# A macaron block with a Mamba-2 mixer on one core: x's rows and Silu earlier in each mixer block

## The chip, the core and the metric

The kernel runs on one core of one Trainium2 chip. The metric is the device time of one launch in microseconds (us), as the median of a few runs. The core has five engines that run their own instruction streams and meet at semaphores: TensorE (PE in the profile, its weight loads PEld), VectorE (DVE), ScalarE (ACT), GpSimd (POOL) and SyncE (SP, which here only issues DMAs).

## The reference

The input is 4 sequences of 512 tokens, 512 wide. Three layers follow each other, each on a layer norm of the residual and each added to it. The first and the last are the same feed-forward (weights turned by Hadamard transforms, 2048 hidden columns, halved output), the one between is a Mamba-2 mixer:

```python
x = x + 0.5 * ffn(layernorm(x))
x = x + mixer(layernorm(x))
x = x + 0.5 * ffn(layernorm(x))

# mixer, cut
gate, xBC, dt = split(h @ in_proj_w.T)
xBC = silu(causal_conv4(xBC) + conv_b)        # x (1024), B (128), C (128)
dt = clip(softplus(dt + dt_bias), 0, 100)     # 64 heads of 16 columns
Y_diag = ((C @ B.T) * exp(segsum(A * dt))) @ (x * dt)     # within a chunk of 64
states = B.T @ (x * dt * decay_to_end)        # per chunk, then carried over chunks
Y_off  = (C @ states) * exp(cumsum(A * dt))
y = (Y_diag + Y_off + D * x) * silu(gate)
out = rmsnorm(y) * norm_w @ out_proj_w.T

# ffn
h = silu(x_gate) * x_up
```

## The kernel before

`begin` turns the weights and runs the first feed-forward of the first sequences. `mixer` is the rest, some 1310 us. Its main loop runs over the 4 sequences (q = 0 to 3) and, within one, over 8 blocks (b = 0 to 7) of 128 x columns, that is 8 heads. Each block also carries one chunk (256 of the 2048 hidden columns) of the feed-forward of another sequence, as filler for TensorE; `at = 8 * q + b` counts both. After block 7 comes a passage that prepares the next sequence; after q = 3, 16 feed-forward chunks are left without a mixer beside them. There are 32 mixer blocks: 8 to a sequence.

Nothing is scheduled at run time. The order of the instructions on each engine is the order in which the loops call the helpers, and each helper waits for the semaphores it needs. Every float32 product of the projections and of the feed-forward is made of three passes of split operands (`PASSES`), so a projection of one 128-column block is 12 matmuls of 128x512.

The helpers that matter here, in TensorE's order in a block of before:

- `x_rows` (L1287): 4 transposes of x's Silu output `xc` into bank X, whose readers on DVE are `scaled` (L1805) and `scaled_end` (L1814)
- `decay` (L1277), four times, each followed by ACT's Exp (L1552), with the four `down` matmul groups of the filler (L1231) between
- `in_proj` (L1146) for the next block's x, `new_states` (L1315), `times_start` (L1322, the product behind the carried exponents), then `up0` and `gate1` of the filler (L1190, 24 matmuls; in block 0 only 12, since `up0` stands earlier)
- `ydiag`, the inner product (L1299, 32 products, each on 32 columns of the array), `from_states`, the product from the states (L1328), `in_proj` for the next block's gate (L1146), `up1`, in odd blocks `out_proj` (L1259), and `gate0` of the next chunk (L1190)

On DVE: `states` (L1831 to L1837), `conv` of the next block (L1791, three steps), `hidden` (L1762), `hidden_low` (L1768), `within` (L1850), `carried` (L1857), and pieces of layer-norm statistics and of the mixer's own norm (L129 to L167) as they come due: `norm` in block 1 of q = 1 to 3, a piece of `other` in block 4 of q = 0 to 2, a piece of `following` in block 6 of every q. On ACT: `times` (L1557, Exp), `x_silu` (L1502), `gate` (L1521) and `silu` (L1537, all Silu), `hidden_high` (L1543), `square` (L1572). Exp and Silu sit in different function tables, so each block has two table loads (ACT_TABLE_LOAD).

Of the kernel before, what the change touches and what calls it, by code (L numbers as in the profile page):

```python
# [862 lines left out]
def mixer(nc, s, ug_s, dn_s, wsc, in_s, out_s, cum_m, cum_s, out):  # L863
# [17 lines left out]
    with ExitStack() as ctx:  # L881
# [233 lines left out]
        def _(pe):  # L1115
# [163 lines left out]
            def x_rows(q, b):  # L1279

                pe.wait_ge(s_xcv, LCONV * q + 2 + b + 1)
                if b == 0:
                    pe.wait_ge(s_gt, q + 1)
                else:
                    pe.wait_ge(s_ex, NB * q + b)
                for i in range(NPC):
                    ins = pe.transpose(X[:, ck(i)], xc[:, b % 2, ck(i)], I)  # L1287
                ins.then_inc(s_X, 1)
# [92 lines left out]
            for q in range(BATCH):  # L1381
                more = q < BATCH - 1
                for b in range(NB):
                    at = NC * q + b
                    end = b == NB - 1
                    pair = last_pair(q, b)
                    x_rows(q, b)
                    decay(q, b, 0)
                    if at == 0:
                        in_proj(q, 5, 0)  # L1390
                        decay(q, b, 1)
                        in_proj(q, 5, 1)
                        decay(q, b, 2)
                        new_states(q, b)
                        decay(q, b, 3)
                    elif b == 0:
                        in_proj(q, 5, 0)
                        decay(q, b, 1)
                        in_proj(q, 5, 1)
                        decay(q, b, 2)  # L1400
                        new_states(q, b)
                        decay(q, b, 3)
                        up0(at)
                    else:
                        down(at - 1, 0, last_pair(q, b - 1) + 1)
                        if end:
                            turn_tile(q + 1, 0)
                        down(at - 1, 1)
                        decay(q, b, 1)
                        down(at - 1, 2)  # L1410
                        if end:
                            turn_tile(q + 1, 1)
                        decay(q, b, 2)
                        down(at - 1, 3)
                        if end:
                            turn_tile(q + 1, 2)
                        decay(q, b, 3)
                        if b == 1 and q:
                            sums(q - 1)
                        if not end:  # L1420
                            in_proj(q, 5 + 2 * b)
                    if b:
                        new_states(q, b)
                    if end:
                        turn_tile(q + 1, 3)
                    times_start(q, b)
                    if b:
                        up0(at)
                    if end and more:
                        in_proj(q + 1, 0)  # L1430
                    if at:
                        gate1(at)
                    if at == 0:
                        gate0(at + 1, 0)
                    ydiag(q, b)
                    from_states(q, b)
                    if not end:
                        in_proj(q, 6 + 2 * b)
                    elif more:
                        in_proj(q + 1, 1)  # L1440
                    if at:
                        up1(at)
                    if pair >= 0:
                        out_proj(pair, at)
                    if at and (not end or not more):
                        gate0(at + 1, pair + 1)
# [3 lines left out]
                at = NC * q + NB - 1  # L1450
# [16 lines left out]
            for at in range(NC * BATCH, NC * ITEMS):  # L1467
                q, b = at // NC, at % NC
# [20 lines left out]
        def _(act):  # L1489
# [165 lines left out]
            for q in range(BATCH):  # L1655
                more = q < BATCH - 1
                for b in range(NB):
                    at = NC * q + b
                    end = b == NB - 1
# [9 lines left out]
                    if not end:  # L1669
                        raw(q, 3 + b, b + 1)  # L1670
                    times(q, b)
                    if at:
                        hidden_high(at, 0)
                    if end and more:
# [3 lines left out]
                    if end and more:  # L1678
                        step_exp(q + 1)
                        raw(q + 1, 0, NB)  # L1680
                    if at:
                        silu(at, 1)
                    if not end:
                        x_silu(q, b + 1)
                        gate(q, b + 1)
                    elif more:
                        b_silu(q + 1)
# [48 lines left out]
        def _(dve):  # L1736
# [214 lines left out]
            for q in range(BATCH):  # L1951
# [3 lines left out]
                for b in range(NB):  # L1955
# [28 lines left out]
                        keep_sums(q - 1)  # L1984
                    if end:
                        turn_tile(q + 1, 3)
                    if b == 4 and more:
                        next(other)
                    if b == 6:
                        next(following)  # L1990
                    states(q, b)
                    if not end:
                        conv(q, 3 + b, b + 1)
                    if at:
                        hidden(at, 0)
                        hidden_low(at, 0)
                    if end and more:
                        step_abs(q + 1)
                        step_one(q + 1)
                        step_rest(q + 1)  # L2000
                    within(q, b)
                    carried(q, b)
                    if end and more:
                        conv(q + 1, 0, NB)
# [195 lines left out]
```

## Time and profile before

| what | value |
|---|---|
| median of 3 runs | 1646.36 us (1646.13 to 1650.44) |
| the profiled execution | 1646.44 us, span 1644.6 us |
| TensorE busy | 98% of the span, granted clock 0.999 |
| DVE, ACT, POOL busy | 63%, 38%, 23% |
| chain that ended last | 74% PE |
| one mixer block | 27.6 us (even), 33.1 us (odd, with `out_proj`) |

The span runs from the first to the last instruction; 1.8 us of the execution lie around it. The page puts busy time, idle time and who ended it beside each line of the kernel. Matmuls overlap in the pipeline, so two starts of successive groups tell more than their durations.

### The profile page before, as it was taken

The numbers are of one execution on the slowest core, as the hardware profiler recorded it, in microseconds if no ns is written. First come the engines' busy times: TensorE is split into PE (matmuls) and PEld (weight loads), VectorE is DVE, ScalarE is ACT, GpSimd is POOL, SyncE is SP. The second block draws the span as 40 slices with busy tenths as digits, with TensorE's granted clock in tenths as the row PEclk, the third lists the DMA queues.
The fourth block names the chain that finished last, engine by engine and source line by source line (L and its number), as shares of the span: only waits on it lengthen the run. The fifth ranks groups of instructions, "written<-read, shape, count | busy, mean of one in ns | idle before, by whom it ended". The sixth has DMA issues, their size and how long they took to land.

```text
span 1644.6 us, 25044 instructions
## 1 busy us (share of the span) xinstructions
PE 1619.7 (98%) x9672; PEld 1312.1 (80%) x9672; DVE 1035.5 (63%) x2022; ACT 626.1 (38%) x934; POOL 379.1 (23%) x298
## 2 busy tenths in 40 slices
PE   6999999999999999999999999999999999999999
PEld 3788888877888778888877888877888878888887
DVE  6544445776677877777776777777775684543333
ACT  4333434463333463333464334265333341122111
POOL 1656663011221212122122122122122121000000
PEclk9999999999999999999999999999999999999999
DMA  9746564754544444454445445445444447566763
GB/s 291 298 148 245 203 222 166 268 183 143 170 156 151 154 162 145 156 168 151 150 146 167 158 148 173 157 129 195 156 156 157 156 126 223 167 181 192 214 203 129
DMA packets 253427, 290.46 MB, mean 177 GB/s; under 512 B 14464, under 2 KB 211200, under 8 KB 244096
## 3 DMA queue, kind: packets, MB, share of 16 engines
q1 hardware_dynamic: 253312, 288.88, 53.8%
q8 instruction: 78, 1.28, 0.3%
q14 instruction: 37, 0.30, 0.1%
HBM read 238.51 MB, written 50.33 MB: 176 GB/s over the span
## 4 chain that ended last, share of the span: by engine, by line
PE 74%; DVE 2%; ACT 1%; issue 1%; DMA 0%; SPq 0%; ACTq 0%; DVEq 0%
PE bank L1190 31%; PE bank L1231 14%; PE bank L1146 12%; PE bank L1259 5%; PE bank L1328 3%; PE bank L1299 2%; PE bank L1315 2%; PE bank L1277 2%; PE bank L1287 1%; PE bank L1322 1%; DVE xT L1749 0%; PE bank L1174 0%; DVE res L1775 0%; PE bank L1156 0%; DMA cum_stay<-m_aS 0%
## 5 line engine op out<-in xcount | busy, mean ns | idle before, releaser
L1190 PE MATMUL bank<-fxT,wj 128*128 128x512 f32 x1752 | 415.2, 390 | 0.0
L1190 PEld LDWEIGHTS bank<-fxT,wj 128*128 128x128 f32 x1752 | 328.6, 188 | 68.6
L1231 PE MATMUL bank<-m_wd,m_hb 128*128 128x512 f32 x1128 | 278.8, 392 | 0.0
L1231 PEld LDWEIGHTS bank<-m_wd,m_hb 128*128 128x128 f32 x1128 | 209.2, 188 | 44.8 <-issue 2.4
L1543 ACT CAST m_hb<-xn 128x512 fp32r<-128x512 f32 x96 | 59.5, 620 | 452.6 <-DVE xn L1762 452.6
L1146 PE MATMUL bank<-xT,wi 128*128 128x512 f32 x900 | 222.9, 395 | 1.6 <-DVE m_cv L1791 0.5
L1146 PEld LDWEIGHTS bank<-xT,wi 128*128 128x128 f32 x900 | 166.1, 188 | 39.6 <-issue 5.1
L1775 DVE TENSOR_TENSOR res<-bank,res 128x512 f32<-128x512 f32 x192 | 132.5, 690 | 83.0 <-PE bank L1231 80.9
L2098 POOL TENSOR_TENSOR m_L<-m_L,m_GT 128x512 f32<-128x512 f32 x36 | 52.7, 1464 | 431.9 <-ACT m_L L1552 431.9
L1762 DVE SCALAR_TENSOR_TENSOR xn<-bank,sc,xn 128x512 f32<-128x512 f32 x96 | 71.8, 747 | 121.7 <-PE bank L1190 121.6
L1537 ACT ACTIVATE xn<-bank,sc 128x512 f32<-128x512 f32 x96 | 66.1, 688 | 146.4 <-PE bank L1190 140.9
L1552 ACT ACTIVATE m_L<-bank 128x512 f32<-128x512 f32 x128 | 76.5, 598 | 83.7 <-PE bank L1277 83.4
L1768 DVE TENSOR_TENSOR m_hb<-xn,m_hb 128x512 fp32r<-128x512 f32 x96 | 66.3, 691 | 53.5 <-ACT m_hb L1543 53.5
L508 PE MATMUL bank<-xT,b_wu 128*128 128x512 f32 x384 | 95.4, 397 | 0.0
L1791 DVE SCALAR_TENSOR_TENSOR m_cv<-bank,pr,m_cv 128x511 f32<-128x511 f32 (+2 forms) x117 | 87.3, 747 | 10.5 <-ACT m_cv L1497 7.7
L508 PE MATMUL bank<-b_xT,b_wu 128*128 128x512 f32 x384 | 92.9, 392 | 0.0
L1259 PE MATMUL bank<-m_wo,m_yh 128*128 128x512 f32 x384 | 90.7, 391 | 0.7 <-ACT xn L1537 0.7
L2125 POOL TENSOR_TENSOR m_ss<-m_ss,m_y 128x512 f32<-128x512 f32 x28 | 36.2, 1294 | 239.6 <-ACT m_y L1572 239.6
L549 PE MATMUL bank<-b_wd,b_hb 128*128 128x512 f32 x384 | 90.9, 392 | 0.0
L508 PEld LDWEIGHTS bank<-xT,b_wu 128*128 128x128 f32 x384 | 71.8, 188 | 17.9 <-DVE xT L722 0.6
L1259 PEld LDWEIGHTS bank<-m_wo,m_yh 128*128 128x128 f32 x384 | 71.6, 188 | 17.7 <-issue 1.9
L508 PEld LDWEIGHTS bank<-b_xT,b_wu 128*128 128x128 f32 x384 | 72.1, 188 | 16.2 <-issue 0.7
(224 smaller groups left out, 2319.2 us busy)
## 6 DMA issues: line engine op xcount, KB each, us to landing
wj<-ug_split SPq DMA_DIRECT2D x167, 512.0 KB, 4.2
m_wd<-dn_split SPq DMA_DIRECT2D x48, 1024.0 KB, 4.8
wi<-in_split SPq DMA_DIRECT2D x76, 512.0 KB, 3.3
ug_split<-b_wu SPq DMA_DIRECT2D x8, 2048.0 KB, 14.3
m_wo<-out_split SPq DMA_DIRECT2D x32, 512.0 KB, 4.1
wi<-ug_split SPq DMA_DIRECT2D x25, 512.0 KB, 4.2
in_split<-b_msp SPq DMA_DIRECT2D x20, 512.0 KB, 4.0
raw<-in_wug SPq DMA_DIRECT2D x8, 1024.0 KB, 7.0
```

The lines of the kernel that those rows point to most:

```text
L508: ins = pe.matmul(U[j][:], wu[c % 2][:, a, k, ck(j)], xT[g][:, b, k, :], start=(k == 0 and i == 0), stop=(k == KH - 1 and i == 2))
L549: ins = pe.matmul(down_bank(n, t)[:], hb[:, n % 2, a, j, ck(t)], wd[c % 2][:, b, j, :], start=(j == 0 and i == 0), stop=(j == 1 and i == 2))
L1146: ins = pe.matmul(to[:], w[:, a, k, :], xT[:, b, k, :], start=(k == 0 and i == 0), stop=(k == KH - 1 and i == 2))
L1190: ins = pe.matmul(to[:], w[:, a, k, :], frm[:, b, k, :], start=(k == 0 and i == 0), stop=(k == KH - 1 and i == 2))
L1231: ins = pe.matmul(F[t % 2][:], hb[:, a, j, ck(t)], wd[:, b, j, :], start=(j == 0 and n == 0), stop=(j == 1 and n == 2))
L1259: ins = pe.matmul(F[1 - t % 2][:], yh[:, (2 * pair + i) % 4, a, ck(t)], wout[i][:, b, :], start=(i == 0 and n == 0), stop=(i == 1 and n == 2))
L1537: act.activation(hf[:, j, :], F[1][:], ACT.Silu, scale=sc[:, at % NC, j:j + 1]).then_inc(s_sil, 1)
L1552: act.activation(L[:, b % 2, j, :], A[:], ACT.Exp).then_inc(s_L, 1)
L1762: dve.scalar_tensor_tensor(hf[:, j, :], F[0][:], sc[:, at % NC, 2 + j:3 + j], hf[:, j, :], ALU.mult, ALU.mult).then_inc(s_h, 1)
L1768: dve.tensor_tensor(hb[:, 1, j, :], hf[:, j, :], hb[:, 0, j, :].bitcast(F32), ALU.subtract).then_inc(s_lo, 1)
L1775: dve.tensor_tensor(r, frm[:], r, ALU.add).then_inc(s_acc, 1)
L1791: ins = dve.scalar_tensor_tensor(to[:, d:SEQ], frm[:, 0:SEQ - d], pr[:, w + 3 - d:w + 4 - d], to[:, d:SEQ], ALU.mult, ALU.add)
```

## The change

In 27 of the 32 blocks (all but the last of each sequence and the very first), `x_rows` for the next block stands right behind `from_states` instead of at the head of the next block, and `ydiag` stands right behind `times_start` instead of behind `gate1`. On ACT, `x_silu` comes straight after `times`, ahead of the filler's second Silu, `hidden_high` and `square`. On DVE, `states` and `conv` come ahead of the statistics pieces of blocks 4 and 6, and `hidden_low` comes behind `within`. No instruction is added or removed.

```diff
 # tensor
-                    x_rows(q, b)
+                    if b == 0 or at == 1:
+                        x_rows(q, b)
@@
                     times_start(q, b)
+                    if at and not end:
+                        ydiag(q, b)
@@
-                    ydiag(q, b)
+                    if at == 0 or end:
+                        ydiag(q, b)
                     from_states(q, b)
+                    if at and not end:
+                        x_rows(q, b + 1)
 # scalar
                     times(q, b)
+                    if at and not end:
+                        x_silu(q, b + 1)
+                        silu(at, 1)
                     if at:
                         hidden_high(at, 0)
@@
-                    if at:
+                    if at == 0:
+                        x_silu(q, b + 1)
+                    elif end:
                         silu(at, 1)
                     if not end:
-                        x_silu(q, b + 1)
                         gate(q, b + 1)
 # vector
+                    states(q, b)
+                    if not end:
+                        conv(q, 3 + b, b + 1)
                     if b == 4 and more:
                         next(other)
                     if b == 6:
                         next(following)
-                    states(q, b)
-                    if not end:
-                        conv(q, 3 + b, b + 1)
                     if at:
                         hidden(at, 0)
+                    if end:
                         hidden_low(at, 0)
@@
                     within(q, b)
+                    if at and not end:
+                        hidden_low(at, 0)
                     carried(q, b)
```

TensorE in an even block of before, from the new states to the first decay of the next block:

```order
L1315 MATMUL bank<-m_xd,m_Bt 128x128 x7
L1322 MATMUL bank<-m_aS,m_i2x 128x512
L1190 MATMUL bank<-fxT,wj 128x512 x24
L1299 MATMUL bank<-m_L,m_xp 32x64 x32
L1328 MATMUL bank<-m_Cf,m_sta 128x64 x7
L1146 MATMUL bank<-xT,wi 128x512 x12
L1190 MATMUL bank<-fxT,wj 128x512 x24
L1287 MATMUL bank<-cs,m_xc 128x128 x4
L1277 MATMUL bank<-m_mvg,m_stn 128x512
```

The same place now:

```order
L1315 MATMUL bank<-m_xd,m_Bt 128x128 x7
L1322 MATMUL bank<-m_aS,m_i2x 128x512
L1299 MATMUL bank<-m_L,m_xp 32x64 x32
L1190 MATMUL bank<-fxT,wj 128x512 x24
L1328 MATMUL bank<-m_Cf,m_sta 128x64 x7
L1287 MATMUL bank<-cs,m_xc 128x128 x4
L1146 MATMUL bank<-xT,wi 128x512 x12
L1190 MATMUL bank<-fxT,wj 128x512 x24
L1277 MATMUL bank<-m_mvg,m_stn 128x512
```

`ydiag` (L1299) moved ahead of the 24 filler matmuls, the four transposes (L1287) moved ahead of the gate's projection and of 24 more.

ScalarE in a block of before, from the carried exponents' Exp to the filler's next Silu, with the semaphores that each row waits for (`ms_cv` is `conv`, `ms_y` is `within`, `gate` and `ms_flo` belong to the filler):

```order
L1557 ACTIVATE m_ex<-bank 128x512 [waits ms_yf,ms_E]
L1543 CAST m_hb<-xn 128x512 [waits ms_fd,ms_fh]
L1572 ACTIVATE m_y<-m_y 128x512 [waits ms_yl]
L1537 ACT_TABLE_LOAD [waits ms_flo]
L1537 ACTIVATE xn<-bank,sc 128x512 [waits gate]
L1502 ACTIVATE m_xc<-m_cv 128x512 [waits ms_cv,ms_y,ms_X]
L1521 ACTIVATE m_zs<-bank 128x512 [waits ms_yf,projected]
```

The same place now (line numbers are those of the changed kernel: L1563 is `times`, L1508 `x_silu`, L1543 `silu`, L1549 `hidden_high`, L1578 `square`, L1527 `gate`):

```order
L1563 ACTIVATE m_ex<-bank 128x512 [waits ms_yf,ms_E]
L1508 ACT_TABLE_LOAD [waits ms_cv,ms_y]
L1508 ACTIVATE m_xc<-m_cv 128x512 [waits ms_X]
L1543 ACTIVATE xn<-bank,sc 128x512 [waits ms_flo,gate]
L1549 CAST m_hb<-xn 128x512 [waits ms_fd,ms_fh]
L1578 ACTIVATE m_y<-m_y 128x512 [waits ms_yl]
L1527 ACTIVATE m_zs<-bank 128x512 [waits ms_yf,projected]
```

The Silu table's load, which stood behind `square`, now stands behind `times`, and `conv` and `within` are waited for ahead of it.

VectorE in block 1 of q = 1 now, where the mixer's norm begins (L1772 is `hidden`, L1860 `within`, L1778 `hidden_low`, L1867 `carried`, L129 and L130 the norm's first steps):

```order
L1772 SCALAR_TENSOR_TENSOR xn<-bank,sc,xn 128x512
L1860 SCALAR_TENSOR_TENSOR m_y<-m_xc,pr,bank 128x512
L1778 TENSOR_TENSOR m_hb<-xn,m_hb 128x512
L1867 TENSOR_TENSOR m_ex<-bank,m_ex 128x448
L129 TENSOR_SCALAR m_rr<-m_rr 128x4
L130 TENSOR_SCALAR m_rr<-m_rr 128x4
```

Before, `hidden_low` stood ahead of `within`; the rest is as it was.

## Rows read from the trace of the kernel before

**Rows 1.** Page, part 1: engine, busy us, share, instructions.

```profile
PE 1619.7 (98%) x9672; PEld 1312.1 (80%) x9672; DVE 1035.5 (63%) x2022; ACT 626.1 (38%) x934; POOL 379.1 (23%) x298
```

**Rows 2.** Timeline, block 3 of q = 1: start us, us, instruction, [idle before, releaser].

```profile
703.55 0.50 PE L1322 MATMUL bank<-m_aS,m_i2x 128*128 128x512 f32 x1
703.89 5.62 PE L1190 MATMUL bank<-fxT,wj 128*128 128x512 f32 x24
...
707.77 2.31 DVE L1791 SCALAR_TENSOR_TENSOR m_cv<-bank,pr,m_cv 128x511 f32<-128x511 f32 x3
709.45 1.10 PE L1299 MATMUL bank<-m_L,m_xp 128*32 128x64 f32 x64
710.48 1.77 PE L1328 MATMUL bank<-m_Cf,m_sta 128*128 128x64 f32 x14
712.06 3.01 PE L1146 MATMUL bank<-xT,wi 128*128 128x512 f32 x12
...
725.85 0.60 PE L1287 MATMUL bank<-cs,m_xc 128*128 128x128 f32 x4
...
726.52 2.91 PE L1231 MATMUL bank<-m_wd,m_hb 128*128 128x512 f32 x12
```

**Rows 3.** Timeline, end of block 4 of q = 2.

```profile
1004.37 2.31 DVE L1791 SCALAR_TENSOR_TENSOR m_cv<-bank,pr,m_cv 128x511 f32<-128x511 f32 x3
...
1004.95 1.77 PE L1328 MATMUL bank<-m_Cf,m_sta 128*128 128x64 f32 x14
1006.79 0.76 PEld L1146 LDWEIGHTS bank<-xT,wi 128*128 128x128 f32 x4 [0.21 <-issue]
```

**Rows 4.** Timeline, two table loads and what the waits beside them were for.

```profile
358.81 0.71 PE L1363 MATMUL bank<-cs,m_L 64*128 64x64 f32 x8
359.60 1.28 ACT L1552 ACT_TABLE_LOAD   x1 [0.29 <-PE bank L1363]
...
368.23 1.28 ACT L1502 ACT_TABLE_LOAD   x1
370.94 2.31 DVE L1791 SCALAR_TENSOR_TENSOR m_cv<-bank,pr,m_cv 128x511 f32<-128x511 f32 x3
373.28 0.63 ACT L1502 ACTIVATE m_xc<-m_cv 128x512 f32<-128x512 f32 x1 [3.77 <-DVE m_cv L1791]
```

**Rows 5.** Timeline, block 0 of q = 2.

```profile
881.15 2.31 DVE L1791 SCALAR_TENSOR_TENSOR m_cv<-bank,pr,m_cv 128x511 f32<-128x511 f32 x3
...
884.24 3.01 PE L1146 MATMUL bank<-xT,wi 128*128 128x512 f32 x12
```

**Rows 6.** Timeline, block 1 of q = 2.

```profile
908.39 2.31 DVE L1791 SCALAR_TENSOR_TENSOR m_cv<-bank,pr,m_cv 128x511 f32<-128x511 f32 x3
...
913.31 0.62 DVE L1857 TENSOR_TENSOR m_ex<-bank,m_ex 128x448 f32<-128x448 f32 x1
...
918.87 0.75 DVE L1762 SCALAR_TENSOR_TENSOR xn<-bank,sc,xn 128x512 f32<-128x512 f32 x1
...
919.67 0.99 PEld L1259 LDWEIGHTS bank<-m_wo,m_yh 128*128 128x128 f32 x5 [0.32 <-DVE xn L1762]
```

**Rows 7.** Page, part 5: line, tiles, count, busy us, mean ns, idle before.

```profile
L1543 ACT CAST m_hb<-xn 128x512 fp32r<-128x512 f32 x96 | 59.5, 620 | 452.6 <-DVE xn L1762 452.6
L1537 ACT ACTIVATE xn<-bank,sc 128x512 f32<-128x512 f32 x96 | 66.1, 688 | 146.4 <-PE bank L1190 140.9
L1768 DVE TENSOR_TENSOR m_hb<-xn,m_hb 128x512 fp32r<-128x512 f32 x96 | 66.3, 691 | 53.5 <-ACT m_hb L1543 53.5
```

**Rows 8.** Timeline, from block 6 to block 7 of q = 2.

```profile
1078.34 1.28 ACT L1552 ACT_TABLE_LOAD   x1
...
1079.63 0.60 ACT L1552 ACTIVATE m_L<-bank 128x512 f32<-128x512 f32 x1
...
1080.28 0.19 PEld L1277 LDWEIGHTS bank<-m_mvg,m_stn 128*128 128x128 f32 x1 [0.63 <-ACT m_L L1552]
```

## The prediction, written before the changed kernel ran

> **What bounds the kernel now.** I read the page's busy shares first: TensorE is busy for 98% of the span, every other engine for less than two thirds [rows 1]. Most of the 25 us in which it is idle lie ahead of the mixer. So a block is as long as TensorE's own stream, and a change of order can only remove small waits of TensorE or add some. I then read the timeline of one block, start of group to start of group [rows 2]. The 24 filler matmuls start 0.34 us after `times_start` and take 5.56 us, 0.23 each; `ydiag` takes 1.03 us to the next group's start, `from_states` 1.58, and nothing idles between. `conv` ends at 710.08, two microseconds before the gate's projection at 712.06, whose bank it has to free. In blocks 4 and 6 a piece of statistics stands ahead of `states` on DVE, so `conv` ends at 1006.68 and the projection's weights wait: 1.84 us after the start of `from_states` where the normal block has 1.58 [rows 2, 3]. That is about 0.27 us, in 7 blocks (4 and 6 of q = 0 to 2, 6 of q = 3).
>
> **ydiag behind times_start.** The same 32 products and the same two changes of the array's tile, one in and one out. The trace has no change from the long matmul of `times_start` to 32-column tiles. Behind the filler, `ydiag` starts 0.06 before the modelled end of the last matmul (703.89 + 5.62 against 709.45); by the same rule it would start at 703.55 + 0.50 - 0.06, 0.44 behind `times_start`, and the filler 1.03 after that, with its first weights exposed as now (0.34 rather than 0.23 to the next). The fillers then run straight into `from_states` without a tile change. Sum to the start of `from_states`: 0.44 + 1.03 + 0.11 + 24 x 0.23 = 7.1, against 6.93 now, whose own first weights (some 0.05 to 0.1) are hidden afterwards. I take 0. Bounds: nothing, or a loss of 0.1 a block, that is 2.4 us in 24; a gain needs the next point's wait to leave room, and it doesn't.
>
> **x's rows earlier.** At the head of a block the four transposes cost 725.85 to 726.52 less the 0.23 that the decay matmul alone takes: 0.44 us [rows 2]. They cost the same 0.44 behind `from_states`. Moved work is neutral where TensorE is bound, except where a later wait is fixed by something else (block 7, below). Their release, though, now comes from a new chain: `conv`, then ACT. DVE's readers of the rows (`scaled`) start earlier, off the path.
>
> **The table load.** This decides the sign. In before, the Silu table is loaded behind `square`, at a time when nobody waits for ACT. Now the load stands between `times` and `x_silu`, and the order puts the waits for `conv` and `within` ahead of it, with only bank X's on the Silu itself. The trace shows both arrangements. Where no wait stands ahead, the load ran at 368.23 while `conv` ended only at 373.25, and the Silu started 0.03 later. Where the wait stands ahead, the load began 0.08 after the product it was waiting for (358.81 + 0.71, then 359.60) [rows 4]. So I take it that the 1.28 us are spent after `conv`. The x rows' weights then come at the end of `conv` + 0.08 + 1.28 + 0.02 + 0.63 + 0.05 (the lag of weights behind `hidden` in block 1: 919.62, 919.67 [rows 6]) = 2.06 us.
>
> - Normal blocks, and 4 and 6, where the statistics now stand behind `conv`: it ends 6.53 after `times_start` [rows 2], the weights come at 8.59. `from_states`, starting at 7.0, would let them start at 8.55. A wait of 0.04 in 21 blocks: +0.8.
> - Block 0 of q = 1 to 3 has only 12 filler matmuls ahead. `conv` ends at 883.46, the weights come at 885.52, and TensorE is there at 884.24 [rows 5]. 1.28 us; I take 1.25 in 3 blocks: +3.8.
> - Block 1 of q = 1 to 3 has the mixer's norm on DVE, a chain of tiny steps between `carried` (ends at 913.93) and the second `hidden` (918.87), and TensorE already waits 0.32 for that `hidden`, less the usual 0.05 [rows 6]. Now `carried` stands behind `hidden_low`, which needs `hidden_high`, which stands behind both Silus on ACT: `conv` ends at 910.70, load until 912.06, x's Silu until 912.70, the filler's (0.69, overlapping by 0.1) until 913.29, `hidden_high` (0.62, overlapping) until 913.81, `hidden_low` (0.69) until 914.53, `carried` until 915.08 [rows 6, 7]. That is 1.15 late, `hidden` too, and TensorE gives back 0.44 of it at the head of the next block: +0.7 in 3 blocks, +2.1.
>
> What is queued behind the load on ACT in other blocks has room: the filler's second Silu ended at 10.37 after `times_start` in before and would end near 9.1 now; `hidden_high` goes from 7.8 to 9.6, and what needs it first is a `down` eight microseconds off.
>
> **Blocks 4 and 6.** The 0.27 goes in 7 blocks: -1.9. What is late next there is the 0.04 above, counted.
>
> **Block 6 to 7.** At the head of block 7 TensorE waits for the first decay's Exp (1079.63 + 0.60), and its next weights start 0.05 later, 0.63 after the ones before [rows 8]. That Exp follows the filler's Silu, two row copies and a table load, a chain fixed by `gate0`'s end. The 0.44 taken out in front of it only lengthens the wait, while block 6 has already paid for the rows: +0.44 in 4 sequences, +1.8. In the other blocks the same Exp has about half a microsecond to spare; after the shift it would release the weights some 0.1 late, and a weight load is given out well ahead of the end of the matmul before it, so that such a delay need not reach the stream. I take 0.3 in all; between 0 and 1.9 (0.1 in 19 blocks).
>
> **Sum.** 0 + 0.8 + 3.8 + 2.1 - 1.9 + 1.8 + 0.3 = +6.9 us on the profiled execution's 1646.44 (span 1644.6 and 1.8 around it), which is the median of 1646.36 to within 0.1. Forecast 1653.3.
>
> SyncE's loads are the same; some are released about a microsecond later, since the fillers end later, and each lands long before its use.
>
> **Rivals.**
>
> A, the load runs ahead: ACT's queue issues it while `conv` still runs. Then x's Silu ends 0.65 after `conv`, block 0 has no wait (weights at 884.16 against 884.24), and block 1's DVE chain keeps its time, so that its present 0.27 wait is covered by the 0.44. Sum: -1.9 + 1.8 - 0.8 + 0.3 = -0.6, that is 1645.8: not slower. It decides if the load starts before `conv` ends. For it speaks 368.23; against it that no wait stood ahead there. Chance 0.14.
>
> B, TensorE pays more: the tile change behind `times_start` costs 0.1 more in 24 blocks (+2.4), and the late first decay 0.1 in 19 (+1.9). 6.9 + 2.4 + 1.6 = +10.9: 1657.3. Nothing in the rows excludes it; chance 0.15.
>
> C, a table switch that costs more than its row. "ScalarE: Activation LUTs", section "What ACT_TABLE_LOAD costs", of the Trainium skill puts a drain of 1380 ns behind the load of 1283 ns. By that rule x's Silu would end 1.38 later in 27 blocks, +37 us: 1690. The row of 1.28 agrees with the load, and the Exp behind the load at 1078.34 starts at 1079.63, 0.01 after its end [rows 8], so the trace doesn't bear the drain out. Chance 0.01.
>
> D, the moved waits pay off: the earlier rows free DVE sooner and take a wait of TensorE that the timeline books as busy. With A's conditions this could give 1640. TensorE's idle time in the mixer is a few microseconds, so there is little to take. Chance 0.03.
>
> The forecast's own case has 0.67 and a range of 1650 to 1656.
>
> **How the numbers follow.** A measurement of this kernel tells 0.3% (4.9 us) from no change, so slower begins at 1651.3. The forecast's case lies beyond it with four parts in five (0.54), B and C do wholly (0.16): 0.69 slower with rounding. Same: the rest of the forecast's case (0.13) and A (0.14), 0.28 with a little of D. Faster: 0.03. The range for 8 in 10 takes A in at the bottom and B at the top: 1645 to 1658.
>
> **What would show it.** In the profile after: ACT's load between `times` and x's Silu starting 0.1 after `conv`; TensorE's weights for the x rows released by ACT, with an idle of over a microsecond in block 0 of three sequences and near nothing elsewhere; the wait for `hidden` in `out_proj` of block 1 grown from 0.3 to about 1; the projection's idle in blocks 4 and 6 gone; the wait at the first decay of block 7 grown from 0.6 to about 1. A load that starts right behind `times` makes the forecast wrong, and a normal block longer than 27.6 us makes it too low.

## The result, and the profile after

The changed kernel is slower: 1657.78 us, median of 4 runs (1657.23 to 1658.45), against 1646.7 of the kernel before beside it. The ratio is 1.0064, with an interval of 1.005 to 1.0077. The profiled execution took 1658.01 us (span 1656.2, granted clock .999 of full speed, as before), so the trace can be read against the span before, 1644.6: there are 11.6 us to find, where 6.9 were forecast.

The busy shares of the page's part 1 tell hardly anything of it:

```profile
PE 1624.2 (98%) x9672; PEld 1313.5 (79%) x9672; DVE 1022.3 (62%) x2022; ACT 625.2 (38%) x934; POOL 377.1 (23%) x298
```

The instructions are the same in number, and still TensorE's busy time grew by 4.5 us [rows 1], so only 7.1 of the 11.6 us stand in the trace as idle time. That matmuls which wait inside a group are booked as busy would explain it; no run shows it by itself. The list of TensorE's waits (line, releaser: us in total, times, longest) shows the new ones. In it L1287 is `x_rows`, L1231 `down`, L1259 `out_proj`, L1277 `decay`, L1772 the filler's `hidden`, L1778 `hidden_low`:

```profile
PE bank L1231 <- DVE m_hb L1778: 4.2, 10, 0.7
PE bank L1287 <- ACT m_xc L1508: 3.3, 3, 1.1
PE bank L1277 <- DMA m_stn<-cum_stay: 1.4, 2, 0.9
PE bank L1259 <- DVE xn L1772: 1.5, 3, 0.5
```

The same list of before has neither of the first two. The view that settles the sizes is the distance from one `times_start` to the next, block by block, in the timelines, taken from the starts of its weight load (PEld L1322). A block thus reaches into the head of the next. Means over q = 1 to 3 (block 4: q = 1 and 2, the sequences with statistics in it), in us:

| | block 0 | 1 | 2 | 3 | 4 | 5 | 6 |
|---|---|---|---|---|---|---|---|
| before | 25.83 | 33.26 | 27.56 | 33.05 | 27.84 | 33.05 | 28.12 |
| after | 27.10 | 33.96 | 28.50 | 33.11 | 28.17 | 33.12 | 28.32 |

Summed over their blocks: block 0 +3.8, block 1 +2.1, block 2 +2.8, block 4 +1.0, block 6 +0.8 (four times), the other moved blocks +0.7 in all. Block 7 of q = 2 is 1.0 longer through a DMA's round trip, the row L1277 above, whose wait goes from execution to execution (0.8 in before, 1.4 here, 2.4 in one experiment that doesn't touch it). Together +12.2; the stretch up to the first `times_start` was 0.7 shorter (365.3 against 366.0), where TensorE's wait for a start-up load fell from 11.5 to 10.5. That leaves about the 11.6 us of the span.

**Block 0.** Timeline of q = 2: start us, us, instruction, [idle before, releaser], as in all timelines below. L1801 is `conv`, L1508 `x_silu`:

```profile
882.25 0.40 PE L1322 MATMUL bank<-m_aS,m_i2x 128*128 128x512 f32 x1
...
884.86 2.30 DVE L1801 SCALAR_TENSOR_TENSOR m_cv<-bank,pr,m_cv 128x511 f32<-128x511 f32 x3
...
887.26 1.28 ACT L1508 ACT_TABLE_LOAD   x1 [3.98 <-DVE m_cv L1801]
888.55 0.63 ACT L1508 ACTIVATE m_xc<-m_cv 128x512 f32<-128x512 f32 x1
...
889.24 0.42 PEld L1287 LDWEIGHTS bank<-cs,m_xc 128*128 128x128 f32 x4 [1.23 <-ACT m_xc L1508]
```

`conv` ends at 887.16. ACT, idle for 4 us, starts the load 0.10 later and the Silu 1.29 after that; TensorE stands for 1.23 us. In [rows 5] it went from `from_states` straight into the projection. The Silu begins 0.01 us behind the load: the drain of 1380 ns that the Trainium skill's "ScalarE: Activation LUTs" ("What ACT_TABLE_LOAD costs") puts there does not show.

**Block 1.** q = 2. L1543 is the filler's Silu, L1549 `hidden_high`, L1778 `hidden_low`, L1867 `carried`, L1772 the second `hidden`:

```profile
915.74 1.28 ACT L1508 ACT_TABLE_LOAD   x1 [5.49 <-DVE m_cv L1801]
917.04 0.63 ACT L1508 ACTIVATE m_xc<-m_cv 128x512 f32<-128x512 f32 x1
917.58 0.67 ACT L1543 ACTIVATE xn<-bank,sc 128x512 f32<-128x512 f32 x1
918.14 0.61 ACT L1549 CAST m_hb<-xn 128x512 fp32r<-128x512 f32 x1
918.78 0.69 DVE L1778 TENSOR_TENSOR m_hb<-xn,m_hb 128x512 fp32r<-128x512 f32 x1 [1.83 <-ACT m_hb L1549]
919.39 0.62 DVE L1867 TENSOR_TENSOR m_ex<-bank,m_ex 128x448 f32<-128x448 f32 x1
...
924.94 0.75 DVE L1772 SCALAR_TENSOR_TENSOR xn<-bank,sc,xn 128x512 f32<-128x512 f32 x1
...
925.74 1.01 PEld L1259 LDWEIGHTS bank<-m_wo,m_yh 128*128 128x128 f32 x5 [0.93 <-DVE xn L1772]
```

The chain conv, load, two Silus, `hidden_high`, `hidden_low`, `carried` runs as forecast, DVE stands 1.83 us in it, and the wait in `out_proj` is 0.93 where it was 0.32 [rows 6].

**Block 2.** This one was not forecast. Here VectorE has `ending` (L1931, the end of the norm of the q before) between `carried` and the second `hidden`; the list of pieces under "The kernel before" doesn't have it. On GpSimd L2138 is `add_squares`, which waits for ACT's `square`, and L2126 and L2128 are `combine`:

```profile
952.76 0.69 DVE L1778 TENSOR_TENSOR m_hb<-xn,m_hb 128x512 fp32r<-128x512 f32 x1 [1.82 <-ACT m_hb L1549]
953.34 1.28 POOL L2138 TENSOR_TENSOR m_ss<-m_ss,m_y 128x512 f32<-128x512 f32 x1 [10.54 <-ACT m_y L1578]
953.37 0.62 DVE L1867 TENSOR_TENSOR m_ex<-bank,m_ex 128x448 f32<-128x448 f32 x1
953.91 5.22 DVE L1931 SCALAR_TENSOR_TENSOR res<-m_acc,m_rr,res 128x512 f32<-128x512 f32 x4
954.58 1.61 POOL L2126 TENSOR_TENSOR m_y<-m_y,m_ex 128x448 f32<-128x448 f32 x1
956.27 1.62 POOL L2128 TENSOR_TENSOR m_y<-m_y,m_zs 128x512 f32<-128x512 f32 x1
959.05 0.74 DVE L1772 SCALAR_TENSOR_TENSOR xn<-bank,sc,xn 128x512 f32<-128x512 f32 x1
...
961.42 1.39 PE L1231 MATMUL bank<-m_wd,m_hb 128*128 128x512 f32 x5 [0.65 <-DVE m_hb L1778]
```

In before, block 2 of q = 2 starts at 937.41, and the same place reads (L1921 is `ending`, L1762 `hidden`):

```profile
947.09 4.70 DVE L1921 SCALAR_TENSOR_TENSOR res<-m_acc,m_rr,res 128x512 f32<-128x512 f32 x4
951.76 0.75 DVE L1762 SCALAR_TENSOR_TENSOR xn<-bank,sc,xn 128x512 f32<-128x512 f32 x1
```

So `ending` begins 9.68 us after the block's start in before and 10.82 (953.91 less 943.09) in after, and takes 0.52 longer; `hidden` begins 14.35 after it in before and 15.96 in after, 1.6 later. Of the 0.52, the first of `ending`'s four steps has 0.53: taken by itself it lasts 0.74 in before and 1.27 here, since `add_squares`, now behind the load and both Silus, still runs until 954.62. `down` needs `hidden`'s low half at once, and TensorE stands 0.65 us for it.

**Block 4.** Of q = 2, behind `carried`. L137 to L139 are the tiny steps of the block's second piece of statistics, which stands where it stood before:

```profile
1015.95 1.29 POOL L2138 TENSOR_TENSOR m_ss<-m_ss,m_y 128x512 f32<-128x512 f32 x1 [11.56 <-ACT m_y L1578]
1016.51 0.75 DVE L137 TENSOR_TENSOR m_mv<-m_mv 128x4 f32<-128x4 f32 x1
1017.20 1.14 POOL L2126 TENSOR_TENSOR m_y<-m_y,m_ex 128x448 f32<-128x448 f32 x1
1017.29 1.07 DVE L138 TENSOR_TENSOR m_mv<-m_mv 128x4 f32<-128x4 f32 x1
1018.40 0.16 DVE L139 SCALAR_TENSOR_TENSOR m_mv<-m_mv 128x4 f32<-128x4 f32 x1
1018.42 1.30 POOL L2128 TENSOR_TENSOR m_y<-m_y,m_zs 128x512 f32<-128x512 f32 x1
1018.60 1.15 DVE L137 TENSOR_TENSOR m_mv<-m_mv 128x4 f32<-128x4 f32 x1
...
1020.30 0.75 DVE L1772 SCALAR_TENSOR_TENSOR xn<-bank,sc,xn 128x512 f32<-128x512 f32 x1
...
1022.68 1.62 PE L1231 MATMUL bank<-m_wd,m_hb 128*128 128x512 f32 x6 [0.33 <-DVE m_hb L1778]
```

The wait for `conv` of [rows 3] is gone, and one of 0.33 in front of a matmul of `down` has come. The second piece takes 3.8 us here (1016.51 to 1020.30) and 3.3 in before (1009.83 to 1013.09): in both it meets `combine`, and here its first step meets `add_squares` as well, 0.75 where it took 0.15.

**Block 6 to 7**, q = 2. L1558 is the first decay's Exp:

```profile
1083.99 1.63 PE L1231 MATMUL bank<-m_wd,m_hb 128*128 128x512 f32 x6 [0.33 <-DVE m_hb L1778]
...
1086.87 0.60 ACT L1558 ACTIVATE m_L<-bank 128x512 f32<-128x512 f32 x1
1087.51 0.19 PEld L1277 LDWEIGHTS bank<-m_mvg,m_stn 128*128 128x128 f32 x1 [0.50 <-ACT m_L L1558]
```

The wait behind the first decay's Exp is 0.50, against the 0.63 of [rows 8]; e7_rows_back tells what it would be without the earlier rows.

### The profile page after: what moved, and what is told of

The parts are those of the page before. It is cut to its first block, busy times and chain, and to the rows that moved or that the text cites. A ratio compares the mean times of both kernels' runs of the same rounds, so it can differ in the third digit from the quotient of the medians.

```text
span 1656.2 us, 25044 instructions
## 1 busy us (share of the span) xinstructions
PE 1624.2 (98%) x9672; PEld 1313.5 (79%) x9672; DVE 1022.3 (62%) x2022; ACT 625.2 (38%) x934; POOL 377.1 (23%) x298
## 3 DMA queue, kind: packets, MB, share of 16 engines
q8 instruction: 78, 1.28, 0.3%
## 4 chain that ended last, share of the span: by engine, by line
PE 62%; DVE 11%; issue 3%; ACT 3%; DMA 0%; SPq 0%; ACTq 0%; DVEq 0%
PE bank L1190 24%; PE bank L1231 14%; PE bank L1146 10%; PE bank L1259 5%; DVE m_cv L1801 2%; PE bank L1328 2%; DVE m_sta L1845 2%; PE bank L1315 2%; DVE m_sta L1847 1%; PE bank L1277 1%; PE bank L1299 1%; DVE res L1931 1%; PE bank L1287 1%; DVE xn L1772 1%; ACT m_hb L1549 1%
## 5 line engine op out<-in xcount | busy, mean ns | idle before, releaser
L1231 PE MATMUL bank<-m_wd,m_hb 128*128 128x512 f32 x1128 | 279.9, 394 | 4.2 <-DVE m_hb L1778 4.2
L1231 PEld LDWEIGHTS bank<-m_wd,m_hb 128*128 128x128 f32 x1128 | 208.3, 188 | 52.9 <-issue 10.7
L1785 DVE TENSOR_TENSOR res<-bank,res 128x512 f32<-128x512 f32 x192 | 132.5, 690 | 112.6 <-PE bank L1231 109.5
L1549 ACT CAST m_hb<-xn 128x512 fp32r<-128x512 f32 x96 | 59.3, 618 | 300.7 <-DVE xn L1772 300.7
L1772 DVE SCALAR_TENSOR_TENSOR xn<-bank,sc,xn 128x512 f32<-128x512 f32 x96 | 71.8, 748 | 116.5 <-PE bank L1190 116.2
L1543 ACT ACTIVATE xn<-bank,sc 128x512 f32<-128x512 f32 x96 | 65.6, 683 | 140.0 <-PE bank L1190 134.5
L1778 DVE TENSOR_TENSOR m_hb<-xn,m_hb 128x512 fp32r<-128x512 f32 x96 | 66.4, 691 | 72.1 <-ACT m_hb L1549 71.6
L1558 ACT ACTIVATE m_L<-bank 128x512 f32<-128x512 f32 x128 | 76.6, 599 | 79.1 <-PE bank L1277 78.8
L2138 POOL TENSOR_TENSOR m_ss<-m_ss,m_y 128x512 f32<-128x512 f32 x28 | 36.2, 1292 | 273.0 <-ACT m_y L1578 273.0
L1801 DVE SCALAR_TENSOR_TENSOR m_cv<-bank,pr,m_cv 128x511 f32<-128x511 f32 (+2 forms) x117 | 87.3, 746 | 10.5 <-ACT m_cv L1503 7.7
L1259 PE MATMUL bank<-m_wo,m_yh 128*128 128x512 f32 x384 | 91.1, 391 | 2.3 <-DVE xn L1772 1.5
L1259 PEld LDWEIGHTS bank<-m_wo,m_yh 128*128 128x128 f32 x384 | 71.6, 188 | 19.7 <-DVE xn L1772 2.8
```

The source lines that it names most:

```text
L1231: ins = pe.matmul(F[t % 2][:], hb[:, a, j, ck(t)], wd[:, b, j, :], start=(j == 0 and n == 0), stop=(j == 1 and n == 2))
L1259: ins = pe.matmul(F[1 - t % 2][:], yh[:, (2 * pair + i) % 4, a, ck(t)], wout[i][:, b, :], start=(i == 0 and n == 0), stop=(i == 1 and n == 2))
L1549: act.copy(hb[:, 0, j, :], hf[:, j, :]).then_inc(s_hi, 1)
L1558: act.activation(L[:, b % 2, j, :], A[:], ACT.Exp).then_inc(s_L, 1)
L1772: dve.scalar_tensor_tensor(hf[:, j, :], F[0][:], sc[:, at % NC, 2 + j:3 + j], hf[:, j, :], ALU.mult, ALU.mult).then_inc(s_h, 1)
L1778: dve.tensor_tensor(hb[:, 1, j, :], hf[:, j, :], hb[:, 0, j, :].bitcast(F32), ALU.subtract).then_inc(s_lo, 1)
```

## The experiments

Each is timed beside the kernel before, and its ratio is to that; it is worked out from the single runs, and is not the quotient of the two medians. Block lengths of all (us, as in the table above; block 5 of e9_spread is of q = 1 and 2):

| | 0 | 1 | 2 | 3 | 4 | 5 | 6 |
|---|---|---|---|---|---|---|---|
| e1_warm | 25.79 | 33.02 | 27.54 | 33.03 | 28.17 | 33.02 | 28.25 |
| e2_late | 27.08 | 33.92 | 29.31 | 33.08 | 27.91 | 33.10 | 28.29 |
| e3_ydiag | 25.84 | 33.25 | 27.59 | 33.08 | 27.84 | 33.08 | 28.10 |
| e4_conv | 25.83 | 33.25 | 27.56 | 33.05 | 28.32 | 33.05 | 27.88 |
| e7_rows_back | 25.84 | 34.38 | 28.52 | 33.08 | 28.17 | 33.08 | 27.85 |
| e8_conv_b6 | 25.83 | 33.25 | 27.56 | 33.05 | 27.83 | 33.05 | 27.88 |
| e9_spread | 25.83 | 33.06 | 27.56 | 33.06 | 27.75 | 33.93 | 28.25 |

### e1_warm: the table is called for before the wait

The changed kernel, with a Silu of one column between `times` and `x_silu`. It waits for nothing of `conv`, so the load runs early.

```diff
+        warm = sb("warm", [P, 1])
 ...
                     if at and not end:
+                        act.activation(warm[:], pr[:, P_DTB:P_DTB + 1], ACT.Silu)
                         x_silu(q, b + 1)
                         silu(at, 1)
```

> The changed kernel with one extra Silu of one column, on constant data, between times and x_silu in the 27 blocks, so that the Silu table is loaded without waiting for conv. Theory (the load behind conv is the cost): the load starts right behind times, x's Silu ends 0.7 after conv; the wait in block 0 of q = 1 to 3 goes (1.25 each, 3.8), block 1 falls from 33.9 to 33.0 and block 2 from 28.5 to 27.6 since carried is 1.2 earlier (2.8 each in three sequences), and 0.04 in the rest; blocks 4 and 6 stay, since there hidden_high waits for the first hidden, not for ACT. About 10 us less than the changed kernel: 1648. Rival (TensorE's stream itself costs more in the new order): all blocks stay as they are, 1657 to 1658. Second rival (the waits of blocks 2 and 4 are VectorE's own work): only blocks 0 and 1 give, 6.7 us less, 1651.

Measured: 1646.86 us, 10 runs, against 1645.55; 1.0002 (0.9993 to 1.0011). Span 1645.4. Block 0 of q = 2 (L1680 is the helper that records the one-column Silu, L1509 `x_silu`):

```profile
880.55 1.28 ACT L1680 ACT_TABLE_LOAD   x1
881.84 0.20 ACT L1680 ACTIVATE m_warm<-pr 128x1 f32<-128x1 f32 x1
882.08 2.31 DVE L1803 SCALAR_TENSOR_TENSOR m_cv<-bank,pr,m_cv 128x511 f32<-128x511 f32 x3
884.50 0.63 ACT L1509 ACTIVATE m_xc<-m_cv 128x512 f32<-128x512 f32 x1 [2.46 <-DVE m_cv L1803]
885.18 0.42 PEld L1288 LDWEIGHTS bank<-cs,m_xc 128*128 128x128 f32 x4
```

The load ends before `conv` starts, the rows' weights have no wait, and blocks 0, 1 and 2 are back where they were, block 1 0.24 below. Blocks 3 and 5 lose their 0.06 and 0.07 too. The span is 10.8 us shorter than the change's 1656.2. So one load, standing behind a wait, carries nearly all of the loss; the earlier rows by themselves cost nothing in those blocks. Block 4 stays long: that is another cause.

### e2_late: the statistics behind hidden_low

The changed kernel, with `ending` in block 2 and the last piece in block 4 moved behind the second `hidden_low`.

```diff
-                    if b == 2 and q:
-                        ending(q - 1)
-                    if b in (3, 4) and more:
+                    if b == 3 and more:
                         next(other)
-                    if b == 4 and more:
-                        bias(1, s_fs)
 ...
                         hidden_low(at, 1)
+                    if b == 2 and q:
+                        ending(q - 1)
+                    if b == 4 and more:
+                        next(other)
+                        bias(1, s_fs)
```

> The changed kernel with two pieces of VectorE's side work put behind the second hidden_low of their block: ending in block 2 of q = 1 to 3, and the last statistics piece with its bias in block 4 of q = 0 to 2. Theory (TensorE's wait at the first down of the next block is for the second hidden_low, which these pieces push back): block 2 falls from 28.5 to 27.65, block 4 from 28.2 to 27.65, blocks 0 and 1 stay at 27.1 and 33.9; about 4.3 us less than the changed kernel, 1653.5. Rival (the wait at that down has another cause, the late conv chain on ACT alone): nothing moves, 1657.8.

Measured: 1659.25 us, 4 runs, against 1645.55; 1.0082 (1.0067 to 1.0097). A miss: not 4 us better than the change but as slow or slower. Block 2 of q = 2 (L1815 is `scaled`, L1785 `add_down`):

```profile
959.57 0.75 DVE L1772 SCALAR_TENSOR_TENSOR xn<-bank,sc,xn 128x512 f32<-128x512 f32 x1 [3.93 <-PE bank L1190]
...
961.62 2.73 DVE L1931 SCALAR_TENSOR_TENSOR res<-m_acc,m_rr,res 128x512 f32<-128x512 f32 x4
964.27 1.72 DVE L1815 TENSOR_TENSOR m_xp<-bank,m_dd 64x256 f32<-64x256 f32 x4
966.02 0.69 DVE L1785 TENSOR_TENSOR res<-bank,res 128x512 f32<-128x512 f32 x1
...
966.76 1.24 PEld L1231 LDWEIGHTS bank<-m_wd,m_hb 128*128 128x128 f32 x6 [1.71 <-DVE res L1785]
```

`hidden` is now free of `ending`: it waits for TensorE's bank. But the next bank that `down` writes is freed by `add_down`, which stands behind `ending` and `scaled`, and the weights of TensorE's next `down` wait 1.71 us for it. In block 4 the smaller piece did gain, 0.26. Block 2 is 1.75 us longer than its old length where the change cost 0.94: there is no slack behind `hidden_low` for `ending`, while ahead of `hidden` VectorE now stands idle for 3.93 us. `ending` belongs into that gap, and e1_warm, which leaves it there and only has `carried` in time, loses nothing in block 2. The run also gives `ending`'s price by itself: 2.73 us for its four steps with GpSimd idle, against 5.22 in the change beside `add_squares` and `combine`.

### e3_ydiag: the inner product's move alone

Before, with `ydiag` behind `times_start`:

```diff
                     times_start(q, b)
+                    if at and not end:
+                        ydiag(q, b)
 ...
-                    ydiag(q, b)
+                    if at == 0 or end:
+                        ydiag(q, b)
```

> The kernel before with only ydiag moved behind times_start in the 27 blocks. Theory: a block grows by 0 to 0.1 us from TensorE's tile changes and nothing else waits, 0 to +2.5 us against before: 1647 to 1649. Rival (this move is what costs): +5 us or more, 1652 and up. In blocks 4 and 6 the wait for conv stays as it was.

Measured: 1646.75 us, 10 runs, against 1645.55; 1.0005 (0.9996 to 1.0015). No block is longer by more than 0.03. The other tile order costs next to nothing; rival B's first half falls.

### e4_conv: states and conv ahead of the statistics alone

Before, with VectorE's order of blocks 4 and 6 as in the change:

```diff
+                    states(q, b)
+                    if not end:
+                        conv(q, 3 + b, b + 1)
                     if b == 4 and more:
                         next(other)
                     if b == 6:
                         next(following)
-                    states(q, b)
-                    if not end:
-                        conv(q, 3 + b, b + 1)
```

> The kernel before with only states and conv put ahead of the statistics pieces in blocks 4 and 6. Theory: the projection's wait of 0.27 to 0.3 in 7 blocks goes and nothing else moves: 1.9 us less than before, 1644.7. Rival (the pieces then run beside GpSimd's work and take longer, 2.7 us rather than 2.1, so the second hidden is late there as in the changed kernel): block 4 grows by 0.3 to 0.6 and the time stays or rises by up to 2 us.

Measured: 1646.61 us, 10 runs, against 1645.55; 1.0009 (0.9999 to 1.0018). Block 6 is 0.24 shorter, as counted in the prediction. Block 4 is 0.48 longer in spite of the gained wait; its new ones, in q = 2 (`times_start`'s weights at 996.86; L1857 is `carried`, L1762 the second `hidden`, L1768 `hidden_low`):

```profile
1008.83 0.62 DVE L1857 TENSOR_TENSOR m_ex<-bank,m_ex 128x448 f32<-128x448 f32 x1
...
1012.63 0.75 DVE L1762 SCALAR_TENSOR_TENSOR xn<-bank,sc,xn 128x512 f32<-128x512 f32 x1
...
1014.06 0.69 DVE L1768 TENSOR_TENSOR m_hb<-xn,m_hb 128x512 fp32r<-128x512 f32 x1 [0.69 <-ACT m_hb L1543]
...
1015.01 1.17 PE L1231 MATMUL bank<-m_wd,m_hb 128*128 128x512 f32 x4 [0.50 <-DVE m_hb L1768]
```

Ahead of `states` the piece lay partly in time in which VectorE had nothing else to do, and put `conv`'s end back by 2.1 us (8.66 after `times_start` in before, 6.54 here). Behind `conv` all of its 2.8 us stand in the path to the second `hidden`: `carried` ends 12.59 after `times_start` and `hidden` starts at 15.77, where before has 11.89 and 15.07. The second piece takes 3.3 us in both. `down` waits. Block 6 has the same late `hidden` (15.77) and the same wait in `down`, but there the first decay's Exp, which TensorE waited for in before [rows 8], now keeps it waiting no more, and the block is shorter all the same.

The change has this edit too, and block 4's loss in it, 0.33, is the same in e1_warm, without the load behind the wait, and in e7_rows_back, without the earlier rows. But it takes another road. `hidden_low` behind `within` saves VectorE a wait of 0.69 for `hidden_high`, so that `carried` ends at 11.93, nearly as in before. The first `hidden`, though, starts at 9.26 as here, against 8.57, and with it `square` and `add_squares` are late by as much, and the second piece runs into `add_squares`: the second `hidden` starts at 15.63.

### e7_rows_back: the change without the earlier rows

The changed kernel, with `x_rows` again at the head of its own block:

```diff
-                    if b == 0 or at == 1:
-                        x_rows(q, b)
+                    x_rows(q, b)
 ...
-                    if at and not end:
-                        x_rows(q, b + 1)
```

> The changed kernel with x_rows back at the head of the next block; x's Silu with its table load stays early on ACT, ydiag stays behind times_start. Theory (two things wait for the load behind conv: TensorE's early rows in block 0, and hidden_high with VectorE's chain behind it in blocks 1 and 2): block 0 of q = 1 to 3 falls from 27.1 to 25.8, since nobody waits for x's Silu so soon; block 1 stays long, near 34.4 (the second hidden is 1.15 late and nothing is given back at the next block's head), block 2 stays 0.5 to 0.9 long, block 4 0.3 to 0.5 long, block 6 is 0.2 shorter than before. About +5 us against before, 1651. Rival (all of the loss hangs on the moved rows): every block returns to before's length, 1646 to 1647.

Measured: 1652.94 us, 4 runs, against 1646.34; 1.0048 (1.0031 to 1.0064). Block 0 is back at 25.84, since nobody waits for the Silu there now. Block 1 is 1.12 longer than before, as its DVE chain is late and nothing is given back at the head of the next block:

```profile
920.19 0.75 DVE L1769 SCALAR_TENSOR_TENSOR xn<-bank,sc,xn 128x512 f32<-128x512 f32 x1
...
921.00 1.01 PEld L1259 LDWEIGHTS bank<-m_wo,m_yh 128*128 128x128 f32 x5 [1.41 <-DVE xn L1769]
```

Block 2 stays 0.96 longer and block 4 0.33, so that neither is caused by the rows; block 6 is 0.27 shorter, so that its +0.2 in the change is the rows' 0.47 less the wait for `conv`. At the head of block 7 (q = 2; L1555 is the first decay's Exp) `down` waits as in the change, but the Exp keeps nobody waiting:

```profile
1079.63 1.63 PE L1231 MATMUL bank<-m_wd,m_hb 128*128 128x512 f32 x6 [0.34 <-DVE m_hb L1775]
...
1082.07 0.60 ACT L1555 ACTIVATE m_L<-bank 128x512 f32<-128x512 f32 x1
1082.71 0.19 PEld L1277 LDWEIGHTS bank<-m_mvg,m_stn 128*128 128x128 f32 x1
```

So the 0.50 in the change is what the earlier rows brought. The profiled execution was the fastest of the four, 1650.79; its blocks are 6.65 longer in sum than those of before, and the stretch ahead of them 2.35 shorter.

### e8_conv_b6: conv ahead of the piece in block 6 alone

Before, and only block 6's piece goes behind `conv`:

```diff
-                    if b == 6:
-                        next(following)
                     states(q, b)
                     if not end:
                         conv(q, 3 + b, b + 1)
+                    if b == 6:
+                        next(following)
```

> The kernel before with states and conv put ahead of the statistics piece in block 6 alone. From the run with blocks 4 and 6: block 6 falls by 0.23 in each sequence, block 4 keeps 27.85; 0.9 us less than before, if block 7 doesn't give it back. A measurement hardly tells 0.9 from nothing; the blocks' lengths do. Rival (the wait comes back in block 7, which hangs on the same statistics through its row copies): block 7 grows by 0.2.

Measured: 1645.11 us, 10 runs, against 1646.34; 0.9998 (0.9988 to 1.0007). The blocks give 0.24 in each of four sequences, 0.9 us, less than the interval can tell. By the block lengths it is the one edit of the change that pays. The rival, 0.2 given back in block 7, is not there in q = 2, where block 7 is as long as in before (52.88); in q = 1 a wait for a DMA hides it.

### e9_spread: can the pieces go elsewhere?

e1_warm, with the last two pieces moved to later places in blocks 4 and 5:

```diff
-                    if b == 4 and more:
-                        next(other)
 ...
-                    if b in (3, 4) and more:
+                    if b in (3, 4, 5) and more:
                         next(other)
-                    if b == 4 and more:
+                    if b == 5 and more:
                         bias(1, s_fs)
```

> The changed kernel with the early table load (the one-column Silu) and with the second and third piece of the other sequence's statistics moved from block 4 to the late places of blocks 4 and 5. Theory: without the middle piece (2.8 us, none of it hidden behind conv) block 4's second hidden is in time and the block falls from 28.2 to 27.6; block 5 has 5.7 us of pieces between carried and the second hidden, of which some 5 fit: 0 to +0.7 there in q = 0 to 2. Against the run with the early load alone -1.7 to 0 us: 1645 to 1647, near or just under the kernel before. Rival (block 4's length comes from the early rows or ydiag, not from VectorE's pieces): block 4 stays at 28.2.

Measured: 1647.53 us, 10 runs, against 1646.34; 1.0012 (1.0 to 1.0023). Block 4 falls to 27.75, 0.1 below before, and block 5 grows by 0.88:

```profile
1041.47 1.00 PEld L1260 LDWEIGHTS bank<-m_wo,m_yh 128*128 128x128 f32 x5 [0.98 <-DVE xn L1774]
```

Against e1_warm, which it is built on, block 4 gains 0.4 and block 5 loses 0.9: a piece ahead of the second `hidden` costs more in `out_proj` of the odd block than it saves before `down` of the even one. Block 4 was expected at 27.6 and block 5 at up to 0.7 more, so both came out a little worse.

## Why the prediction was right in sign and too low in size

The result lies in the range for 8 in 10 (1645 to 1658), at its top, and outside the 1650 to 1656 of the forecast's own case: the terms that were worked out hold, and two blocks behaved otherwise.

**The table load: right.** It starts 0.10 after `conv` in block 0, and TensorE's weights wait 1.23 in each of three blocks, which grew by 1.27: +3.8 forecast, +3.8 measured. e1_warm takes the load out of the path and the time goes with it; e7_rows_back keeps the load, takes away its first reader, and block 0 is whole. Rival A's mechanism, a load that runs ahead, is real, but needs an instruction ahead of the wait. Given that, the kernel comes out at 1646.86, close to the 1645.8 it was priced at, but not term by term: block 4 costs +1.0 there, where the price has a gain.

**Block 1: right.** +2.1 forecast, +2.1 measured, wait 0.32 to 0.93. The second `hidden` of block 1 is 1.13 late where 1.15 was forecast. The 0.44 given back at the next block's head is what e7_rows_back lacks (+1.12 instead of +0.70).

**The other blocks: right within 0.1 each.** 0.04 in a normal block was forecast and 0.06 to 0.07 came (blocks 3 and 5). The working has a slip: its sum to the start of `from_states` is 7.1, and it goes on with 7.0. Measured are 7.07 (block 1, 916.19 less 909.12), and with 7.1 the forecast would have had no wait there at all. The late first decays, taken at 0.3 in all, cost nothing that shows: e1_warm moves them as well and has blocks 3 and 5 at 33.03 and 33.02, below before.

**Block 2: the step that failed.** The prediction said of what is queued on ACT behind the load that it has room, because what needs `hidden_high` first is a `down` eight microseconds off. That was the path of `hidden_high` alone. `hidden_low` stands ahead of `carried` on VectorE, and behind `carried` in block 2 stands `ending`, 4.7 us, ahead of the second `hidden`, whose `down` does not have eight microseconds. `carried` ends 1.14 later, `ending` takes 0.52 more beside `add_squares`, and `hidden` is 1.6 late. The term was costed at 0.04 a block, +0.1; it measured +2.8. e1_warm, which removes only the load's place, brings block 2 back to 27.54; e7_rows_back, without the earlier rows, leaves it at 28.52. Block 1 was worked out by just this chain; block 2 has the same chain with another piece in it, and was not followed. A normal block over 27.6 had been named as the sign that the forecast was too low.

**Block 4: the gain that turned into a loss.** Of the -1.9 for the waits behind `conv`, block 6's part is right: -0.24 where -0.27 was forecast (e4_conv, e8_conv_b6). Block 4's was taken as -0.7, with the 0.04 counted, and measured +1.0. The question "what is late next" was answered for TensorE's projection alone; what was late next was the second `hidden`, behind pieces that had lain partly in idle time. e4_conv shows it without the rest; in the change the delay comes through `add_squares` instead, from the same edit.

The two blocks have one bound. From the start of `times_start`'s weights, the second `hidden` starts at 15.16, 15.63, 15.77 or 15.96 (block 4 of e9_spread, of the change and of e4_conv, block 2 of the change, q = 2), and the block is 27.75, 28.17, 28.32 or 28.50 long: 12.5 to 12.6 more each time. Where it starts at 14.8 (e1_warm, block 2) the block has its normal length. By that the normal length of 27.56 would be left at 15.0 (an estimate from these rows), and before has `hidden` at 14.35: some 0.6 us of room, not eight.

**Block 6 to 7: right, with a wait overlooked.** -0.27 + 0.04 + 0.44 was forecast per sequence, 0.20 measured. The wait at the first decay did not grow from 0.63 to 1; it is 0.50. The runs take it apart: in e4_conv, e8_conv_b6 and e7_rows_back, with `conv` early and the rows where they were, `down` waits 0.3 to 0.5 for `hidden_low` just ahead and the wait at the decay is gone; with the rows early (the change, e1_warm) it is back at 0.5, and the block 0.47 longer than in e7_rows_back. What the forecast overlooked is `down`'s wait, which takes the place of the old 0.63.

**ydiag: right.** 0 forecast, 0.03 a block at most (e3_ydiag). Rival B's time of 1657.3 was near the result, but neither of its mechanisms is there: the time was right for another reason, block 2 and block 4.

With block 2's +2.7 and block 4's +1.7 more than forecast, +6.9 becomes +11.3, and the median moved by 11.1. The term of block 2 was taken from the path of one reader, and that of block 4 from the wait that it removes; both failed in the same way, at the second `hidden`. What is left open: e1_warm is 0.3 longer in block 4 and 0.13 in block 6 than before. Undoing block 4's order in e1_warm, with block 6's kept, was not tried; by the blocks it would be worth 1.0 us, and e8_conv_b6, the best of the runs by its blocks, could not be told from before.

## What to carry to other kernels

A table load goes out behind the waits of the activation that needs it. If a reorder makes the first activation of another set wait for a late product, the load's 1.28 us are added to that product's path; a one-column activation of the same set ahead of the wait takes them off for 0.20 us of an idle engine.

When a chain is late by x on one block, follow it in every block that has other work in the same gaps: "room" belongs to one reader of one instruction, and the in-order neighbours behind it (here `ending` behind `carried` behind `hidden_low`) have their own deadlines. An engine at 62% over the span can be the bound in two blocks of eight. What a moved piece costs there is set by the idle time at its new place: behind `hidden_low` a small piece of statistics gained 0.26 us and `ending` lost 0.8 (e2_late), and a piece more in block 5 lost 0.9 for 0.4 gained in block 4 (e9_spread).

## What the runs showed of the hardware

Beside GpSimd, VectorE's smallest steps took seven times their length. In block 4 after, L138 ran from 1017.29 to 1018.36 and GpSimd's L2126 ended at 1018.34; the next L137 ended at 1019.75 and L2128 at 1019.72. Alone these steps take 0.16. L139 between them took its 0.16. In the traces of before and of the change the mixer has 61 such steps of 128x4 that take over 0.5 us, and every one ends 0.01 to 0.03 behind a GpSimd tensor operation. Most have two inputs; L131 in block 1, a step with one input, took 1.00. The Trainium skill has the rule ("SBUF — State Buffer", section "SBUF: two separate sides"): the port pair that both engines share is an exclusive lock for the whole instruction, taken on VectorE's side by operations with two SBUF inputs, among others. The trace agrees with it. Four steps of 128x512, 2.73 us with GpSimd idle, took 4.70 and 5.22 beside it, and the first step, which meets `add_squares` in the second case, makes the difference of the two. GpSimd pays as well: L2126 takes 1.14 in block 4 and 1.61 beside `ending`.

The other surprise was how cheap the change of tile shape is: 64 matmuls with 32-column tiles moved between two streams of full-width matmuls cost at most 0.03 us a block.
